# The first block's scan in two halves of the state, with one sum of five terms and the outputs made 16 pairs at a time on GpSimd, TensorE and ScalarE

## The reference, cut to what matters

```python
def step(S, inp):
    r_, w_, k_, v_, kk_, b_ = inp
    sab = jnp.einsum('bhvk,bhk->bhv', S, kk_)
    S = S * jnp.exp(w_)[:, :, None, :] + sab[..., None] * b_[:, :, None, :] + v_[..., None] * k_[:, :, None, :]
    y = jnp.einsum('bhvk,bhk->bhv', S, r_)
    return (S, y)
_, y = jax.lax.scan(step, S0, (rh, wh, kh, vh, kkh, bh))
```

## Time and profile before

| what | value |
| --- | --- |
| median of three runs | 3112.15 us |
| the profiled execution's own time | 3108.21 us |
| its span in the profile | 3106.5 us |
| VectorE busy over the span | 2271.5 us (73%) |
| TensorE matmul, ScalarE, GpSimd busy | 2370.6, 1673.8, 930.1 us |
| the scan, from its first to the end of its last state | 362.44 to 758.36 us |

### The profile page before, as it was taken

The page is one execution under the profiler, slowest core; times in us unless marked ns, Lnnn a source line. Parts: engine busy times, 40 slices in busy tenths (PEclk is TensorE's granted clock), DMA queues, the critical chain, the costliest instruction groups (busy, mean ns, idle before and its releaser), DMA issues. The chain is left out here.

```text
span 3106.5 us, 36881 instructions
## 1 busy us (share of the span) xinstructions
PE 2370.6 (76%) x10040; PEld 999.9 (32%) x10040; DVE 2271.5 (73%) x6009; ACT 1673.8 (54%) x3015; POOL 930.1 (30%) x938
## 2 busy tenths in 40 slices
PE   6665344452697999777999989977877888868887
PEld 2121243341253434333333333322332111224343
DVE  6999599997675665465656555658748999757776
ACT  4444333330564666462212118855568999777775
POOL 0222555652044555211000005410011000028886
PEclk8777556655897999889999999988988999989999
DMA  3112665422366656323011004310013111101110
GB/s 124 54 55 68 151 115 104 87 33 46 97 223 123 125 117 116 85 105 82 26 31 31 26 16 96 93 30 0 1 44 92 43 46 44 27 27 37 38 41 24
DMA packets 295844, 211.34 MB, mean 68 GB/s; under 512 B 155321, under 2 KB 263785, under 8 KB 295145
## 3 DMA queue, kind: packets, MB, share of 16 engines
q1 hardware_dynamic: 257696, 191.80, 23.7%
q0 software_dynamic: 19712, 14.96, 3.7%
q10 hardware_dynamic: 18256, 2.52, 0.5%
HBM read 136.18 MB, written 62.52 MB: 64 GB/s over the span
## 5 line engine op out<-in xcount | busy, mean ns | idle before, releaser
L2953 ACT ACTIVATE ca_pw<-ca_ps,ca_mx 128x512 f32<-128x512 f32 x512 | 342.8, 930 | 10.2 <-DVE ca_mx L2989 10.2
L2827 DVE CUSTOM_DVE_ANT_0 mx_sums<-mx_ps,w_w2f 128x512 f32<-128x512 f32 (+3 forms) x512 | 220.4, 486 | 153.6 <-PE mx_ps L2805 153.6
L2989 DVE TENSOR_REDUCE ca_mx<-ca_ps 128x1 f32<-128x512 f32 x512 | 311.4, 677 | 2.0 <-PE ca_ps L2919 2.0
L2784 PE MATMUL gm_ps<-gm_h,w_w2f 128*128 128x512 f32 x512 | 245.4, 612 | 0.0
L2953 ACT ACTIVATION_READ_ACCUMULATOR ca_pw<-ca_ps,ca_mx 128x1 f32 x512 | 230.0, 449 | 0.0
L2919 PE MATMUL ca_ps<-qs,ks 128*128 128x512 bf16 x512 | 175.9, 396 | 50.3 <-ACT ca_pw L2953 33.1
L2515 ACT ACTIVATE ta_pw<-ta_ps,w_cst 128x1280 f32<-128x1280 f32 x128 | 168.0, 1322 | 35.3 <-PE ta_ps L2396 35.0
L2859 ACT ACTIVATE gm_h<-gm_ps,w_w2f 128x512 f32<-128x512 f32 x64 | 44.0, 688 | 253.1 <-PE gm_ps L2784 253.1
L2654 DVE TENSOR_TENSOR ta_pw<-ta_pw,w_cst 128x384 f32<-128x384 f32 x128 | 70.7, 553 | 135.9 <-ACT ta_pw L2515 133.2
L2234 ACT ACTIVATE at_pw<-at_ps 128x1280 f32<-128x1280 f32 x128 | 154.8, 1236 | 28.1 <-PE at_ps L2199 28.1
L615 PE MATMUL ex_hps<-ex_xgt,ex_w 128*128 128x128 f32 x384 | 87.2, 398 | 96.5 <-ACT ex_xgt L783 96.2
(11 more groups left out here) (577 smaller groups left out, 6268.7 us busy)
## 6 DMA issues: line engine op xcount, KB each, us to landing
Pd<-s_p SPq DMA_DIRECT2D x64, 384.0 KB, 2.6
ex_w<-e_w SPq DMA_DIRECT2D x48, 256.0 KB
Qd<-rp_q SPq DMA_DIRECT2D x4, 2048.0 KB, 9.6
ss_ellb<-Rd SPq DMA_DIRECT2D x32, 256.0 KB, 3.5
ta_qs<-Pd SPq DMA_DIRECT2D x32, 192.0 KB
ta_ks<-Pd SPq DMA_DIRECT2D x32, 192.0 KB
GX<-Qd SPq DMA_DIRECT2D x44, 128.0 KB
SX<-Qd SPq DMA_DIRECT2D x33, 128.0 KB
```

The source lines that it names most:

```text
L2784: last = pe.matmul(mps[:, f, :], W(("h1", "h2")[n - 2])[:, j * 512 + f * 128:j * 512 + (f + 1) * 128], src[:, j, :], start=(j == 0), stop= ...
L2827: last = v.tensor_tensor_reduce(out=sums[:, u, at:at + n], in0=ps[:, u, at:at + n], in1=K["w2f"]("down")[:, T - n:T], scale=-1.0, scalar=3 ...
L2953: act.activation(pw[:, h % BUF, jk, :], ps[:, (h * NB + jk) % BANKS, :], ACT.Exp, bias=mx[:, h % H, jk:jk + 1], accum_out=z[:, h % H, jk:j ...
L2989: v.tensor_reduce(mx[:, h % H, jk:jk + 1], ps[:, q % BANKS, :], AX.X, ALU.max, negate=True).then_inc(S["top"], 1)
```

## The change

The state is cut into rows v 0 to 3 and v 4 to 7, and every step of a pair is issued for one half and then the other: `kkd` (the state times two key rows and the decay, 96 elements, L710 after), `sa` (64 elements into 8, L718), `outer` (64 elements, L721) and `sum` (160 elements into 32, L727). There are again eight instructions per pair. All terms of a pair lie in `run`, one slot of 64 elements per term; `kkd` fills slots 0 to 2, `outer` slots 3 and 4, GpSimd's two products slots 5 and 6, and the sum takes slots 2 to 6. The slot is the outermost axis, so the five terms of one element lie 64 words (256 bytes) apart, and the sum reads them with its innermost step over the slots. All writes of a pair are unbroken runs. GpSimd no longer adds the two products.

The states of 8 pairs stay in a PSUM bank; there are two banks. ScalarE copies a full bank to `hist` in SBUF (`copy_out`), GpSimd multiplies 16 states by the two output rows (`output`, 1024 elements each), writing every element 1 KB from the one before, TensorE sums over k with eight products with the unit matrix (`sums`), and ScalarE copies the result into `y` (`keep`). For the last 16 pairs VectorE makes one of the two products. The experts' PSUM tiles shrink: `tps` and `yps` from two buffers to one, `hps` from three to two.

```diff
+        st = ctx.enter_context(nc.psum_tensor("rs_st", [128, 2, 8, N, N], F32))
+        sa = ctx.enter_context(nc.psum_tensor("rs_sa", [128, 512], F32))[:, 0:2 * N].rearrange("p (h s v) -> p h s v", h=2, s=2)
+        run = ctx.enter_context(nc.sbuf_tensor("rs_run", [128, 2, 2 * HP + 5, N, N], F32))
+        hist = K["XN"][:, 0:2 * HP * N * N].rearrange("p (l m v k) -> p l m v k", l=2, v=N, k=N)
+        prod = K["XN"][:, 2 * HP * N * N:4 * HP * N * N].rearrange("p (k e m v) -> p k e m v", k=N, e=2, v=N)
+        yops = ctx.enter_context(nc.psum_tensor("rs_yo", [128, 512], F32))
+        yo = yops[:, 0:2 * HP * N]
...
+        def slot(n, q):
+            return run[:, n % 2, 5 + q:5 + q + 2 * HP - 1:2]
+        def turned(n, e):
+            return prod[:, :, e].rearrange("p k m v -> p m v k")
 
...
+            def output(n, e):
+                g.wait_ge(Y["hist"], 2 * (n + 1))
+                g.wait_ge(Y["yo"], n)
+                g.tensor_tensor(turned(n, e), hist[:, n % 2], broad(n, RR + e), ALU.mult).then_inc(Y["out"], 1)
...
+            fetch(0)
+            second_product(0)
+            for n in range(LOTS):
+                if n + 1 < LOTS:
+                    fetch(n + 1)
+                    first_product(n + 1)
+                add(n, 0)
+                if n + 1 < LOTS:
+                    second_product(n + 1)
+                add(n, 1)
+                if n:
+                    output(n - 1, 0)
+                add(n, 2)
+                if n:
+                    output(n - 1, 1)
+            output(LOTS - 1, 0)
+            g.wait_ge(X["added"][EL - 1], 16 * (LOTS // TURN))
...
+            def sums(n):
+                pe.wait_ge(Y["out"], 2 * (n + 1))
+                pe.wait_ge(Y["yev"], n)
+                for k in range(N):
+                    last = pe.matmul(yo, cst("ident"), prod[:, k].rearrange("p e m v -> p (e m v)"),
+                                     start=(k == 0), stop=(k == N - 1))
+                last.then_inc(Y["yo"], 1)
...
+            def slots(n, q, many, half):
+                at = n % HP * 2 + q
+                return run[:, n // HP % 2, at:at + many, half * V4:half * V4 + V4]
+            def given(n, q, many):
+                here = lay[:, n // CP % LANES, n % CP, q:q + many, :]
+                return here.unsqueeze(2).to_broadcast([128, many, V4, N])
...
+                for half in range(2):
+                    if n:
+                        done("sum", n - 1, half)
+                    else:
+                        v.wait_ge(Y["zeroed"], 1)
+                    v.tensor_tensor(slots(n, 0, 3, half), state(n - 1, half).unsqueeze(1).to_broadcast([128, 3, V4, N]),
+                                    given(n, KK, 3), ALU.mult).then_inc(step, 1)
+                for half in range(2):
+                    done("kkd", n, half)
+                    if half and n and n % HP == 0:
+                        v.nop().then_inc(S["used"][1 - lot % 2], 1)
+                    if half and n and n % 8 == 0:
+                        v.nop().then_inc(S["full"][1 - n // 8 % 2], 1)
+                    v.tensor_reduce(sa[:, half], slots(n, 0, 2, half), AX.X, ALU.add).then_inc(step, 1)
+                for half in range(2):
+                    done("sa", n, half)
+                    v.tensor_tensor(slots(n, 3, 2, half), sa[:, half].unsqueeze(3).to_broadcast([128, 2, V4, N]),
+                                    given(n, BB, 2), ALU.mult).then_inc(step, 1)
+                for half in range(2):
+                    done("outer", n, half)
+                    if n % 8 == 0 and n >= 16 and not half:
+                        v.wait_ge(Y["hist"], n // 8 - 1)
+                    v.tensor_reduce(state(n, half), slots(n, 2, 5, half).rearrange("p s v k -> p v k s"), AX.X,
+                                    ALU.add).then_inc(step, 1)
+            done("sum", PAIRS - 1, 1)
+            v.nop().then_inc(S["full"][1], 1)
+            v.wait_ge(Y["hist"], 2 * LOTS)
+            v.wait_ge(Y["yo"], LOTS - 1)
+            v.tensor_tensor(turned(LOTS - 1, 1), hist[:, (LOTS - 1) % 2], broad(LOTS - 1, RR + 1), ALU.mult).then_inc(Y["out"], 1)
 
         @block.scalar
...
+            for n in range(LOTS):
+                if n:
+                    copy_out(n - 1, 1)
+                if n + 2 < LOTS:
+                    lay_out(n + 2)
+                if n >= 3:
+                    keep(n - 3)
+                if n + 1 < LOTS:
+                    experts_in(n + 1)
+                copy_out(n, 0)
+                if n + 1 < LOTS:
+                    experts_out(n + 1)
+            copy_out(LOTS - 1, 1)
+            for n in range(LOTS - 3, LOTS):
+                keep(n)
...
+            def copy_out(n, part):
+                act.wait_ge(S["full"][part], n + 1)
+                if n >= 2:
+                    act.wait_ge(Y["out"], 2 * (n - 1))
+                act.activation(hist[:, n % 2, part * 8:part * 8 + 8].rearrange("p m v k -> p (m v k)"),
+                               st[:, part].rearrange("p m v k -> p (m v k)"), ACT.Copy).then_inc(Y["hist"], 1)
+            def keep(n):
+                a, i = n // 2 % LANES, n // 4
+                act.wait_ge(Y["yo"], n + 1)
+                if n % 2 == 0:
+                    act.wait_ge(S["stored"][a], 16 * i)
+                for e in range(2):
+                    last = act.activation(y[:, a, :, e, n % 2 * HP:n % 2 * HP + HP].rearrange("p v m -> p m v"),
+                                          yo[:, e * HP * N:(e + 1) * HP * N].rearrange("p (m v) -> p m v", v=N), ACT.Copy)
+                last.then_inc(Y["yev"], 1)
+                if n % 2:
+                    act.wait_ge(Y["yev"], n + 1)
+                    act.dma_start(Yd[:, :, :, n // 2 * CP:(n // 2 + 1) * CP], y[:, a]).then_inc(S["stored"][a], 16)
```

More of the change, by code:

```diff
@@ L441, in scan_and_experts_phase @@
     Qd, Yd = K["Qd"], K["Yd"]
-    N = 8
+    N, V4 = 8, 4
     R = 64 + E
     Qh = Qd.rearrange("q b (h n) t -> q (b h) n t", n=N)
[L445 to L448, removed]
+    HP = CP // 2
+    LOTS = M // HP
+    EL, EG = 12, 3
+    TURN = EL // EG
     part = lambda a: slice(64 * a, 64 * a + E)
     with ExitStack() as ctx:
-        S = sems(nc, ctx, "rs", "loaded laid steps stored", LANES)
-        V = sems(nc, ctx, "rsv", "first second vk used", 2)
+        S = sems(nc, ctx, "rs", "loaded laid stored full first second used", 2)
+        Y = sems(nc, ctx, "ry", "hist out yo yev zeroed")
@@ L633, in _ @@
+            sums(LOTS - 2)
+            sums(LOTS - 1)
         @block.vector
@@ L743, in _ @@
-            end = counts[SEG - 1]
-            v.wait_ge(chain[SEG - 1], end)
-            sums(PAIRS - 2).then_inc(chain[SEG - 1], 1)
-            output(PAIRS - 1, 0).then_inc(chain[SEG - 1], 1)
-            output(PAIRS - 1, 1).then_inc(chain[SEG - 1], 1)
-            v.wait_ge(chain[SEG - 1], end + 3)
-            sums(PAIRS - 1).then_inc(chain[SEG - 1], 1)
-            v.wait_ge(chain[SEG - 1], end + 4)
-            v.nop().then_inc(S["steps"][1], 1)
+            v.tensor_tensor(slot(0, 0), tall(0, VV), broad(0, KV), ALU.mult).then_inc(S["first"][0], 1)
@@ new lines, in _, with count, done, state @@
+            PAIRS = LOTS * HP
+            names = ("kkd", "sa", "outer", "sum")
+            def count(name, n, half):
+                return n % CP * 8 + names.index(name) * 2 + half + 1
+            def done(name, n, half):
+                v.wait_ge(chain[n // CP], count(name, n, half))
+            def state(n, half):
+                return st[:, n // 8 % 2, n % 8, half * V4:half * V4 + V4]
+            def slots(n, q, many, half):
+                at = n % HP * 2 + q
+                return run[:, n // HP % 2, at:at + many, half * V4:half * V4 + V4]
@@ new lines, in experts_in @@
+            def experts_in(n):
+                i = n // TURN
+                for e in group(n):
+                    act.wait_ge(X["tps"][e], i + 1)
+                    act.wait_ge(X["hps"][e], i)
+                    act.activation(xgt[:, e, :], tps[:, 0:CAP], ACT.Copy).then_inc(X["xgt"][e], 1)
+                for e in group(n):
+                    act.wait_ge(X["hps"][e], i + 1)
+                    act.wait_ge(X["yps"][(e - EG) % EL], i + (e >= EG))
+                    for s in range(S4):
+                        at = (n * EG + e % EG) * S4 + s
+                        last = act.activation(h[:, e % EG, s, :], hps[:, e % 2, s, :], ACT.Gelu, bias=b1[:, at:at + 1])
+                    last.then_inc(X["h"][e], 1)
@@ L800, in _, with experts_out @@
+            def experts_out(n):
+                i = n // TURN
+                for e in group(n):
+                    of = n * EG + e % EG
+                    act.wait_ge(X["yps"][e], i + 1)
+                    act.wait_ge(X["added"][e], 16 * i)
+                    act.activation(ye[:, e, :], yps[:, 0:C], ACT.Copy, scale=WGT[:, of:of + 1]).then_inc(X["y"][e], 1)
             first_columns(act, K, slice(EARLY, 128), S["loaded"][0], range(1, USED, 2))
```

324 lines of the change are left out of this document (95 added, 229 removed).

## The result

The changed kernel takes 3130.18 us (median of 4 runs, 3128.37 to 3133.78) against 3112.55 for the kernel before in the same session (4 runs, 3111.12 to 3113.14): a ratio of 1.0059, with a 95% interval of 1.0041 to 1.0076. It is slower, by 17.6 us. The profiled execution took 3129.64 us itself, 21.4 more than that of before.

A forecast was written before the change was run, and what follows sets the result against it. The prediction took VectorE's queue, by elements and instruction count, to bound the scan. Terms +7.0, -2.9 and +13.1 gave +17.2 us: 3125.4 against the execution's own 3108.2, 3129 us as a median, range 3112 to 3143.

The forecast's parts named there:

- VectorE's pair, +7.0: Scan: the sum's stepped read costs 1.79 ns per element, so the scan takes 402.9 us instead of 395.9.
- ScalarE 19.5 under 25.0, cost 0: Scan: ScalarE's 19.5 us of work per 16 pairs hides under VectorE's 25.0 us and adds nothing.
- waits are covered: Scan before the change: other instructions fill VectorE's waits for results, 0.33 us for the keys sum's wait.
- the stage goes by elements and by the number of instructions: Scan: VectorE's element and instruction counts set its length, 1.54 us per pair, 394 us for 256 pairs.
- the prediction's own line: VectorE's start distance per instruction in the scan: 0.065 us plus 1.05 ns per element.
- Start, -2.9: First products before the scan: VectorE's work there shrinks, so the first pair starts at 359.5 us, not 362.44.
- End, +13.1: After the last state: copies, sums and products of the last lots run serially, 14.2 us against 1.1 before.
- never more than 4.5: End: upper bound in us for TensorE's eight products of 256 columns for one lot; 3.6 was taken.
- The stepped read is free: Rival on VectorE's sum: its stepped read costs nothing extra, scan 342.5 us, program 3069 us; chance 0.28.
- Free, but another engine takes over: Rival on the scan: read free, but ScalarE's lot of 22.5 us exceeds VectorE's 21.4, program 3087 us; chance 0.08.
- 2.49 ns: Rival on the sum: its read costs ScalarE's stepped-write rate per element, scan 460.2 us, program 3187 us; chance 0.09.
- The end costs little: Rival on the end: lot 14 done before the last state, end +5, program 3121 us; within the 0.05 for anything else.

The follow-up runs named there:

- e1: Changed kernel, but the sum of five reads 160 words lying side by side, leaving the recurrence out: 3114.56 us, ratio 1.0001 to the kernel before.
- e7: Kernel before with the output products and output sums taken off VectorE, nothing in their place, outputs stored as zeros: 3107.47 us, ratio 0.9993.
- e6: Changed kernel without the halves, each of a pair's four steps issued once over the whole state: 3192.2 us, ratio 1.0263 to the kernel before.
- e10: e1 with ScalarE's copy of finished sums put ahead of the next lot's lay-out, recurrence left out: 3069.7 us, ratio 0.9877 to the kernel before.
- e4: Changed kernel with ScalarE's copies of lots 13 and 14 put ahead of its copy of the last states: 3125.51 us, ratio 1.0036.
- e2: Changed kernel, but the sum reads five words 352 bytes apart from the inputs, recurrence left out: 3156.88 us, ratio 1.0138 to the kernel before.
- e5: Changed kernel with three ScalarE queue moves, those of e3, e4 and e10 together: 3115.59 us, ratio 1.0022 to the kernel before.
- e3: Changed kernel with ScalarE's first copy of states put ahead of the experts of group 1: 3127.64 us, ratio 1.0051 to the kernel before.
- e8: e5 with the five terms side by side, keys in a dense tile, decay its own instruction, fewer expert-row buffers: 3104.09 us, ratio 0.9988.

## Why the prediction was right

The forecast of 3129 us is 1.2 under the result, and that closeness is partly luck. In the profiled executions the change cost 21.4 us where the sum said 17.2; the medians differ by 17.6, because this execution lay 0.5 under its median and the one before 3.9. By its terms:

- **VectorE's pair, +7.0: measured +6.1, of other parts.** The chosen value, a stepped read that pays what L664's write pays, was right in kind: e1 against the changed kernel shows it. The rate is 1.73 ns per element, not 1.79. The figure 1.73 of the Trainium skill ("Vector Engine (DVE) Microarchitecture Reference", section 5.2) agrees with this trace. The full rate that the same section of the Trainium skill reports for a one-source program did not hold for this sum. That section of the Trainium skill also says that small steps cost more than large ones; between 64 and 88 words the runs show the contrary, 1.73 and 2.04, and the measurement decides. The 256 pairs so came 11 us under the term (1.52 against 1.56 each). That was made up by luck: by the wait of 6.7 us, by the pairs that carry signals (one in eight takes 0.1 or 0.2 us longer, 5 us over the scan where I had 3), and by about 1 us of small spread in the other pairs. That wait was nowhere in the working. The prediction said that a VectorE wait on `hist` would make it wrong there even if the total fits, and so it is: the step "ScalarE 19.5 under 25.0, cost 0" compared work per lot and not the place of each copy in the queue.
- **The premise "waits are covered", "the stage goes by elements and by the number of instructions": half wrong.** e7 removes three of eight instructions and the pair stays. The kernel before stood at both limits at once: by the prediction's own line its eight instructions with 960 elements need 1.53 us (an estimate), and the chain takes 1.54. The sum came out right because the changed pair does go by its instructions. Along one half's chain the durations (247, 218, 218 and 427 ns) and four hand-overs make 1.23 to 1.31 us, an estimate that is under 1.52. e1 shows it: with each sum 0.11 shorter the pair fell by both of them, 0.21.
- **Start, -2.9: measured -1.8.** From the first product to the first pair it took 3.25 us instead of 5.97, 2.7 less; but the first product itself began 0.9 later (357.38 for 356.47). That 0.9 is not an effect of the change as far as the runs tell: the same product starts between 356.84 and 360.00 in e1 to e6 and e10, and at 357.75 in e7, whose code up to there is nearly that of before.
- **End, +13.1: measured +15.6.** The chain was as described, piece by piece. TensorE's two lots were under-sized: 5.13 and 5.41 us instead of 3.6. The step that failed is the reading of the earlier trace rows, which are not eight products of 512 columns. The profile counts two matmuls for one fp32 product: L600 issues eight products and shows x16, and L310 issues two products for each of two lanes and shows x8. So the earlier trace rows are four products, 2048 columns in 4.53 us, and eight products of 256 columns are 2048 columns too: there was nothing to halve, and "never more than 4.5" was no bound. The rest is the clock: it was granted at 0.79 in the earlier trace rows, at 0.71 and 0.69 in the two stretches, and at 0.54 in e4, where the same lot took 6.78 us. `keep` took 0.6 for a lot and not 1.0, GpSimd's product 3.97 and not 3.6.
- **The rivals.** "The stepped read is free" is false. Had it been true, it would have given 3115 (e1) and not 3069, since the circle of queue orders would have taken its place. "Free, but another engine takes over" named a limit of 22.5 us per lot; the real one was 24.1, made of waits and not of work. "2.49 ns" was not reached; e2 shows that part of the way to it is real. "The end costs little" failed as argued: ScalarE's order kept lot 13's copy behind the last states, and e4 and e5 took 4.5 and 5.9 us out of it by that order. But its own price of +5 was too low: with lot 14 out of the way, the end of e5 is still 10.8 us, +9.7.

What stays open: why the step of 352 bytes costs more than 256, and whether the tile has a part in it; and why the same code reaches the first product up to 3 us earlier or later from run to run, which is as much as e3 gained.

## What to carry to other kernels

Before moving work off the engine that looks busy all the time, check if the distance from start to start equals the duration of each instruction plus the hand-over along the chain of results: if so, the work to be removed is hidden, as the outputs were here, and taking it away gains nothing by itself. Cutting a dependent chain into two halves taken in turn paid here, but not with a layout that made the largest read a stepped one. Before a row is scaled to other work, its count is to be held against the calls in the code: here two matmuls in the profile were one product. Work moved to other queues needs its place in them checked lot by lot, in the first and the last lot above all, and a circle over two queues (who releases whom, in what order) is a limit like any engine's work, although no engine in it looks busy.

## What the runs showed of the hardware

- A VectorE sum of 160 elements into 32: 318 ns unbroken, 427 with each element 256 bytes from the last, 476 with 352 bytes. In start distance the first two are 0.23 and 0.34 us: the stepped read is paid in full, unlike the stepped writes of L720 and L730 (64 and 128 elements), of which L730's cost 96 ns of duration and 20 ns of start distance.
- A 64-element product of VectorE written every 20 bytes took 267 ns instead of 218 (e8, L725) and 0.155 us of start distance instead of 0.135.
- The output product of 1024 elements on GpSimd (L573) took 3.97 us beside VectorE's 1.90 us product and 2.36 to 2.97 in the lots of the changed kernel's scan.
- VectorE waiting for its own result starts 0.03 to 0.05 us after that result is complete (e6, e7).
- One fp32 product on TensorE shows as two matmuls. 2048 columns of such products took 4.53 us at a granted clock of 0.79, 5.13 at 0.71, 5.41 at 0.69 (the changed kernel) and 6.78 at 0.54 (e4).
